# The last sample's way through the end of a ternary layer: its rotation in another bank and earlier, its addition by VectorE, unread matmuls in TensorE's waits

## The reference, cut to what matters

```python
def _L3_xattn_ref(x, w1, w2):                      # w1 = w2 = ctx_1024, 77 rows per sample
    h = jnp.einsum('eth,efh->etf', x, w1)
    a = jax.nn.gelu(h, approximate=True)
    return jnp.einsum('etf,efh->eth', a, w2)
...
    xh = x @ H                                     # Hadamard rotation, 256 x 256
    xq = _quantize_activations(xh)                 # scale = max|row| / 7, round, times scale
    wq = _ternary_quantize_ste(weight)
    return jnp.einsum('bsi,oi->bso', xq, wq)
...
x = x + _L3_xattn_ref(_layernorm(x, axis=-1), ctx_1024, ctx_1024)
x = x + _L3_ffn_ref(_layernorm(x, axis=-1), L3_ffn_weight)
return x
```

## Time and profile before

| | us |
|---|---|
| median of three runs | 1186.24 |
| the three runs | 1185.79, 1186.24, 1193.78 |
| the profiled execution | 1185.42 |
| its span in the profile | 1183.7 |
| TensorE busy (matmuls) in that span | 1104.3 |
| VectorE busy | 768.8 |
| ScalarE busy | 429.0 |
| GpSimd busy | 524.4 |

### The profile page before, as it was taken

The page is one execution under the profiler, slowest core; times in us unless marked ns, Lnnn a source line. Parts: engine busy times, 40 slices in busy tenths (PEclk is TensorE's granted clock), DMA queues, the critical chain, the costliest instruction groups (busy, mean ns, idle before and its releaser), DMA issues.

```text
span 1183.7 us, 20960 instructions
## 1 busy us (share of the span) xinstructions
PE 1104.3 (93%) x7481; PEld 928.5 (78%) x7481; DVE 768.8 (65%) x1714; ACT 429.0 (36%) x886; POOL 524.4 (44%) x502
## 2 busy tenths in 40 slices
PE   9999999999899997999979999999998899989995
PEld 5788888886778765988878999999996688875663
DVE  5899889988887447889732222222224888787783
ACT  3454533335555311111112222222222356553464
POOL 5554224447776122758665110100373665431352
PEclk9999999999999997998968999999999799998998
DMA  6999600002000200000146231211221100000001
GB/s 227 395 395 386 247 1 1 18 6 82 5 1 1 64 37 1 1 1 32 41 143 245 106 141 73 107 39 36 80 62 45 55 10 1 1 1 1 2 27 45
DMA packets 44181, 93.60 MB, mean 79 GB/s; under 512 B 3885, under 2 KB 17998, under 8 KB 41414
## 3 DMA queue, kind: packets, MB, share of 16 engines
q1 hardware_dynamic: 35702, 62.24, 14.6%
q0 software_dynamic: 7104, 29.14, 6.9%
q10 hardware_dynamic: 1296, 1.18, 0.3%
HBM read 39.02 MB, written 51.51 MB: 76 GB/s over the span
## 4 chain that ended last, share of the span: by engine, by line
PE 53%; issue 21%; DVE 14%; POOL 4%; ACT 4%; SPq 2%; DMA 1%; POOLq 1%; PEldq 0%; ACTq 0%; DVEq 0%; PEld 0%
PE PS L2361 12%; PE PS L2371 11%; PE PS L1080 7%; PE PS L1093 3%; PE PS L1058 3%; PE PS L1048 2%; DVE scr L1427 2%; PE PS L1601 2%; DVE scr L1453 2%; PE PS L1006 2%; SPq L383 1%; POOL big L676 1%; DVE big L1340 1%; PE PS L1087 1%; DVE scr L404 1%
## 5 line engine op out<-in xcount | busy, mean ns | idle before, releaser
L2394 ACT ACTIVATE scr<-PS,W 128x128 f32<-128x128 f32 x148 | 53.5, 367 | 192.2 <-PE PS L2361 191.1
L2361 PEld LDWEIGHTS PS<-scr 128*128 128x128 f32 x992 | 118.2, 194 | 5.0 <-issue 1.7
L2361 PE MATMUL PS<-scr 128*128 128x128 f32 x992 | 120.2, 279 | 1.3 <-ACT scr L2389 1.3
L708 POOL TENSOR_TENSOR scr<-scr,small 128x1232 f32<-128x1232 f32 x32 | 71.9, 2246 | 101.8 <-DVE small L459 101.7
L2371 PE MATMUL PS<-scr 128*128 128x256 f32 x496 | 112.2, 379 | 0.0
L2424 DVE TENSOR_SCALAR scr<-PS,W 128x128 f32<-128x128 f32 x148 | 51.2, 350 | 82.2 <-PE PS L2361 82.2
L846 ACT ACTIVATE big<-PS 128x512 f32<-128x512 f32 x144 | 73.9, 524 | 82.9 <-PE PS L1058 81.9
L2371 PEld LDWEIGHTS PS<-scr 128*128 128x128 f32 x496 | 91.8, 190 | 11.2
L2430 DVE TENSOR_TENSOR scr<-PS,W 128x256 f32<-128x256 f32 x37 | 15.7, 425 | 125.7 <-PE PS L2371 118.3
L1058 PE MATMUL PS<-W,scr 128*128 128x128 f32 x480 | 78.9, 283 | 9.9 <-ACT big L824 3.0
L1080 PEld LDWEIGHTS PS<-scr,big 128*128 128x128 f32 x640 | 81.0, 191 | 8.1 <-issue 5.1
(11 more groups left out here) (416 smaller groups left out, 2492.8 us busy)
## 6 DMA issues: line engine op xcount, KB each, us to landing
expert_in<-zeros SPq DMA_DIRECT2D x1, 19712.0 KB, 60.6
expert_out<-zeros SPq DMA_DIRECT2D x1, 19712.0 KB, 113.0
scr<-ew_in POOLq DMA_DIRECT2D x12, 1024.0 KB, 6.2
scr<-expert_in SPq DMA_DIRECT2D x38, 128.0 KB
big<-ew_in POOLq DMA_DIRECT2D x4, 1024.0 KB, 8.2
expert_out<-scr POOLq DMA_DIRECT2D x28, 128.0 KB, 2.0
W<-pack SPq DMA_DIRECT2D x1, 2458.0 KB, 8.9
W<-pack SPq DMA_DIRECT2D x1, 2152.0 KB, 8.4
```

Of the source, the lines that this page charges most:

```text
L708: g.tensor_tensor(sc3, sc3, a_mx[u % 3].unsqueeze(2).broadcast_to([P, H, S2]), ALU.subtract).then_inc(s["sub_ready"], 1)
L2361: ins = pe.matmul(bank(1 + f % 4, G), e_w1[slot][:, k, f * P:(f + 1) * P], e_xT[:, k, :], start=(k == 0), stop=(k == C - 1))
L2394: a.activation(e_h[:, f, :], bank(1 + f % 4, G), ACT.Relu, bias=moe_bias(e, f)).then_inc(s["h_act"], 1)
```

## The change

`ROT_BANKS` names the bank of each sample's rotation: 5 as before for the first seven, 0 for the last. TensorE's rotation becomes a function, `rotated`. For the last sample it is called in iteration 8 right behind the turn of that sample, ahead of the transposition of sample 6's quantised rows, and it no longer waits for the quantising of sample 6. That wait moves to VectorE's reciprocal, which overwrites `h_inv`. On ScalarE the copy of bank 4 to the rows of `X` moves, for the last sample, from behind the kept turn to behind the narrowing of sample 6. In iteration 8 TensorE gets unread matmuls in bank 1: four ahead of the turn, two behind it, eight behind the product of sample 6. The last sample's addition goes from GpSimd (`finished`) to VectorE (`last_finished`).

```diff
--- before.py
+++ after.py
@@ -2874,6 +2874,8 @@
             a.activation(h_w3T, bank(0).bitcast(BF16)[:, 0:C * D].rearrange("p (c n) -> p c n", c=C), ACT.Copy)
             a.activation(h_row, bank(1, D), ACT.Copy).then_inc(tail["wT_ready"], 1)
 
+        ROT_BANKS = [5] * (B - 1) + [0]
+
         def tail_dve(v, ch):
             s = tail
 
@@ -2943,8 +2945,10 @@
 
             def rotated(i):
                 v.wait_ge(s["rot_psum"], i + 1)
-                ch.link(v.tensor_reduce(h_am, bank(5).rearrange("p (t d) -> p t d", t=T), AX.X, ALU.max, apply_absolute_value=True))
+                ch.link(v.tensor_reduce(h_am, bank(ROT_BANKS[i]).rearrange("p (t d) -> p t d", t=T), AX.X, ALU.max, apply_absolute_value=True))
                 ch.link(v.tensor_scalar(h_sc[i % 2], h_am, 1e-5, 1.0 / 7.0, ALU.max, ALU.mult))
+                if i == B - 1:
+                    v.wait_ge(s["q_ready"], 2 * i - 1)
                 v.reciprocal(h_inv, h_sc[i % 2]).then_inc(s["am_ready"], 1)
 
             def ternary(i):
@@ -2955,6 +2959,12 @@
                     ins = v.scalar_tensor_tensor(out=h_y[i % 2][:, t, :], in0=bank(7, D, t * D), scalar=h_sc[i % 2][:, t:t + 1],
                                                  in1=h_row, op0=ALU.mult, op1=ALU.mult)
                 ins.then_inc(s["y3_used"], 1)
+
+            def last_finished(i):
+                v.wait_ge(*at("y3_used", i + 1))
+                v.wait_ge(s["x2_ready"], i + 1)
+                v.wait_ge(s["x_ready"], i)
+                v.tensor_tensor(rows(i), rows(i), h_y[i % 2], ALU.add).then_inc(s["x_ready"], 1)
 
             v.wait_ge(gates["tanh_ready"], 1)
             magnitudes(0)
@@ -2977,6 +2987,7 @@
                     rotated(j - 2)
                 if 0 <= j - 3 < B:
                     ternary(j - 3)
+            last_finished(B - 1)
 
         def tail_pool(g):
             s = tail
@@ -3004,7 +3015,7 @@
                     rstd_of("f", j - 1)
                 if j + 1 < B:
                     rstd_of("s", j + 1)
-                if 0 <= j - 3 < B:
+                if 0 <= j - 3 < B - 1:
                     finished(j - 3)
 
         def tail_act(a):
@@ -3034,6 +3045,7 @@
                     turned("c", j)
                 if 1 <= j <= B:
                     turned("f", j - 1)
+                if 1 <= j < B:
                     a.activation(rows(j - 1), bank(4).rearrange("p (t d) -> p t d", t=T), ACT.Copy).then_inc(s["x2_ready"], 1)
                 if j == 0:
                     onehots_kept(a, 1, 0, 5)
@@ -3046,10 +3058,12 @@
                     i = j - 2
                     a.wait_ge(*at("am_ready", i + 1))
                     for t in range(T):
-                        ins = a.activation(h_q[:, t, :], bank(5, D, t * D), ACT.Identity, bias=h_round[:, 0:1], scale=h_inv[:, t:t + 1])
+                        ins = a.activation(h_q[:, t, :], bank(ROT_BANKS[i], D, t * D), ACT.Identity, bias=h_round[:, 0:1], scale=h_inv[:, t:t + 1])
                     ins.then_inc(s["q_ready"], 1)
                     a.wait_ge(s["q_ready"], 2 * i + 1)
                     a.activation(h_qb, h_q, ACT.Identity, bias=h_round[:, 1:2]).then_inc(s["q_ready"], 1)
+                    if j == B:
+                        a.activation(rows(B - 1), bank(4).rearrange("p (t d) -> p t d", t=T), ACT.Copy).then_inc(s["x2_ready"], 1)
                     a.wait_ge(s["qT_psum"], i + 1)
                     a.activation(h_qT, bank(3, S, S).bitcast(BF16).rearrange("p (c s) -> p c s", c=C),
                                  ACT.Copy).then_inc(s["qT_ready"], 1)
@@ -3083,6 +3097,14 @@
                         ins = pe.transpose(bank(2 if kind == "c" else 6, P, c * S + t * P), z[:, t, c * P:(c + 1) * P], ident)
                 ins.then_inc(s[kind + "_psum"], 1)
 
+            def rotated(i):
+                pe.wait_ge(*at("f_ready", i + 1))
+                for t in range(T):
+                    for c in range(C):
+                        ins = pe.matmul(bank(ROT_BANKS[i], D, t * D), f3_zT[:, c, t * P:(t + 1) * P], had[:, c, :],
+                                        start=(c == 0), stop=(c == C - 1))
+                ins.then_inc(s["rot_psum"], 1)
+
             pe.wait_ge(*at("os_ready", 1))
             onehots_turned(pe, 0, 2)
             clocked(pe, 5, 3)
@@ -3092,8 +3114,14 @@
             for j in range(B + 2):
                 if j < B:
                     turn("c", j)
+                if j == B:
+                    pe.wait_ge(*at("y_used", B))
+                    clocked(pe, 1, 4)
                 if 1 <= j <= B:
                     turn("f", j - 1)
+                if j == B:
+                    clocked(pe, 1, 2)
+                    rotated(B - 1)
                 if j == 0:
                     pe.wait_ge(gates["onehot_ready"], 2)
                     onehots_turned(pe, 1, 5)
@@ -3126,15 +3154,10 @@
                             ins = pe.transpose(bank(3, S, S).bitcast(BF16)[:, c * S + t * P:c * S + (t + 1) * P],
                                                h_qb[:, t, c * P:(c + 1) * P], identb[:, :])
                     ins.then_inc(s["qT_psum"], 1)
-                if 1 <= j <= B:
-                    i = j - 1
-                    pe.wait_ge(*at("f_ready", i + 1))
-                    if i:
-                        pe.wait_ge(s["q_ready"], 2 * i - 1)
-                    for t in range(T):
-                        for c in range(C):
-                            ins = pe.matmul(bank(5, D, t * D), f3_zT[:, c, t * P:(t + 1) * P], had[:, c, :], start=(c == 0), stop=(c == C - 1))
-                    ins.then_inc(s["rot_psum"], 1)
+                if 1 <= j < B:
+                    if j > 1:
+                        pe.wait_ge(s["q_ready"], 2 * j - 3)
+                    rotated(j - 1)
                 if 0 <= j - 2 < B:
                     i = j - 2
                     pe.wait_ge(s["qT_ready"], i + 1)
@@ -3144,6 +3167,8 @@
                         for c in range(C):
                             ins = pe.matmul(bank(7, D, t * D), h_qT[:, c, t * P:(t + 1) * P], h_w3T[:, c, :], start=(c == 0), stop=(c == C - 1))
                     ins.then_inc(s["y3_psum"], 1)
+                if j == B:
+                    clocked(pe, 1, 8)
 
         def out_sp(sp):
```

## The result

| | runs | median, us | lowest to highest |
|---|---|---|---|
| before | 10 | 1188.32 | 1185.33 to 1193.83 |
| changed | 10 | 1179.57 | 1173.90 to 1185.21 |

A forecast was written before the change was run, and what follows sets the result against it. Most of the kernel is TensorE-bound, the changed end bound by one serial chain. Gain 3.77 + 0.65 + 0.61 - 0.12 = 4.9 us: span 1178.8, profiled execution 1180.5, plus 0.82 for the median gives 1181.3 us; range 1178.8 to 1186.0.

The forecast's parts named there:

- Order: Rotation of sample 7 ahead of sample 6's transposition on TensorE: quantising 7 starts 3.77 us earlier, 1.20 of it clock.
- Clock and unread matmuls: Unread matmuls on TensorE keep full clock to the end: transposition and product gain 0.65 us; the last eight cost 0.12.
- the 1.20 and 0.65 that I booked as clock: Full-clock gains for sample 7 on TensorE: 1.20 us in the rotation, 0.65 in the last transposition and product.
- the premise beside it: TensorE's clock falls only in gaps over 2 us; gaps left are under 0.7, so full clock to the end.
- Addition: Last sample's addition on VectorE instead of GpSimd: 0.72 us against 1.33 including the link, a gain of 0.61.
- The worse bound: VectorE's last addition takes 1.128 us, as in another stage, instead of 0.69; the move then gains 0.17 us.
- Sum: Chain of sample 7 to the last addition's end: 1176.25 against 1181.17, a gain of 4.9 us.
- End stretch: Time from the start of sample 7's turn on TensorE to the last addition's end; 14.63 us in the kernel before.
- the half clock from the rotation on: Rival, 0.13 in part or wholly: clock falls when sample 7's rotation starts; gain 0.7 us, 1185.5.
- the slower case: Rival, 0.02: TensorE at half rate from the first unread matmul, the eight ending late; 0.2 to 0.8 us slower.
- a late GpSimd: Rival, 0.05 with sample 6's store: GpSimd's addition for 6 ends last, 1.9 us late; gain 3 us or less, 1183.5.

The follow-up runs named there:

- all seven executions: Profiled executions with all three bursts of unread matmuls in the new order, the changed kernel's two and five variants: rotation 1.99 us, product of sample 7 0.61.
- the meeting that I made: Changed kernel with GpSimd's addition for sample 6 held until sample 7's scaling, VectorE's last addition not waiting for it: VectorE 0.69 us, GpSimd 1.77, 10.88 from sample 7's turn.
- the second: Kernel before and changed kernel measured once more with no edit: 1186.39 us and 1182.21 us, ratio 0.9962.

## Why the prediction was right

**Order.** Forecast: rotation 1.33 us after the turn starts, quantising 7 at 4.45. Measured: 1.34 and 4.50. Sample 6 stayed hidden as worked out (its kept rows done 4.19 after the turn, quantising 7 at 4.50).

**Clock and unread matmuls.** Rotation 1.99 (forecast 1.95), last product 0.61, last transposition right behind the eight, at 6.42 (forecast 6.39). The gain was right. The changed kernel's trace can't test how it divides; the experiments do. In the old order the unread matmuls are worth 2.0 us, in the new one 0.5 to 0.8 (10.26 and 10.58 us without them), because the new order by itself closes the long waits: order and addition without any unread matmul already give 4.1 to 4.4 of the 4.9. Less the addition's 0.62, the order alone (with the copy's move) gives 3.4 to 3.8, where I booked 2.57 for it (3.77 less 1.20). The two parts don't add; much of the 1.20 and 0.65 that I booked as clock can be had by either. What failed is the premise beside it, that falls come only in gaps over 2 us: the clock fell about the end of a gap of 1.5, and in a rotation behind gaps of 1.2 and 0.8. The trace of before could have told me: behind its wait of 1.91 us in iteration 1 the granted clock was 0.50 (from 1105 to 1106 us), and the score product took 1.91 us in place of 1.09. It did no harm here, since the filled stretch, whose gaps are none over 0.7, kept the clock in all seven executions.

**Addition.** 0.61 forecast, 0.62 measured. The worse bound was misread: 1.128 us is a mean of additions of 0.69 and of 1.57, so the bound was 1.57, and with it the move would have lost 0.27 us (1.33 less 1.60) in place of gaining 0.17. It takes GpSimd's addition to start just ahead, which `last_finished` rules out by its wait; in the meeting that I made, VectorE was ahead and wasn't held.

**Sum.** End stretch 9.71 forecast (1176.25 - 1166.54), 9.74 and 9.75 measured; gain 4.92 against 4.89. The forecast time of 1181.3 lies between the changed kernel's two medians, 1179.57 and 1182.21. That the measured 1179.57 lies in my range at all is in part luck: the first comparison moved by 8.75 us (1188.32 - 1179.57), the second by 4.18 (1186.39 - 1182.21), and my range ended at 1178.8. What I put too small is the spread: I took 0.5 us between the lower runs of before as its size, and the leads of single executions differ by up to 8.7 us. Of the rivals, the half clock from the rotation on showed up in the kernel without unread matmuls, for less than I priced, since it came back sooner; the slower case and a late GpSimd showed nowhere.

## What to carry to other kernels

At the end of a program one sample's chain is all there is, so an instruction of another sample that stands ahead of it in an engine's order is paid in full: put the last chain first, in a buffer of its own, and check that the other sample still fits behind it. Unread matmuls cost nothing while nothing is due behind them and their full 0.216 us each once something is, so size them to the wait (eight here, by 0.1 us too many). Don't add their gain to that of a new order before each has been measured without the other (here 2.0 us alone, 0.5 to 0.8 on top). Before a mean is taken as a bound, read the single instructions behind it. Where a change is worth less than the run-to-run spread, compare a stretch from a fixed instruction to the end in two traces, not the spans.

## What the runs showed of the hardware that was not expected

The mean granted clock and the span of the same program differ between executions. The changed kernel, by the view of its core's span and mean granted clock:

```profile
core 0: 1175.9 us, clock 0.968
```

and again, by the same view:

```profile
core 0: 1180.2 us, clock 0.961
```

The second span is 4.3 us longer, at 0.007 less of mean clock, with no instruction changed. I had read two falls in one trace as a rule on gaps; it takes several executions of the same program to see that the fall moves, once into the rotation (2.81 us) and once behind it (1.97).
